# A decoder block's first stage: how the denominators of the rational softmax are inverted

## What is computed

```python
def rational_softmax(scores, eps=EPS):                     # EPS = 1e-6
    num = 0.5 * (1.0 + scores * jax.lax.rsqrt(1.0 + scores * scores))
    return num / (jnp.sum(num, axis=-1, keepdims=True) + eps)
...
scores = jnp.where(causal[None, None], NEG, scores + alibi)
probs = rational_softmax(scores, EPS)
out = jnp.einsum('bhts,bhsd->bhtd', probs, v)
out = jnp.transpose(out, (0, 2, 1, 3)).reshape(B, T, C)
return out @ w_out.T                                       # added to x
```

## Time and profile before

| | |
|---|---|
| median of three runs | 3285.65 us |
| the profiled execution | 3286.76 us |
| its span, first to last instruction | 3284.9 us |
| TensorE busy, share of the span | 3043.6 us, 93% |
| VectorE busy | 1644.6 us, 50% |
| ScalarE busy | 1347.1 us, 41% |
| GpSimd busy | 733.1 us, 22% |
| TensorE's granted clock, mean | 0.962 |

### The profile page before, as it was taken

How to read it: one execution, slowest core, us unless ns; L and a number is a source line. 1 busy time by engine, 2 the same in 40 slices (tenths; PEclk the granted TensorE clock), 3 DMA queues, 4 the chain that set the end, 5 groups by cost and what they waited for, 6 DMA issues and landing times. The chain is left out here.

```text
span 3284.9 us, 50660 instructions
## 1 busy us (share of the span) xinstructions
PE 3043.6 (93%) x19312; PEld 2491.3 (76%) x19312; DVE 1644.6 (50%) x3785; ACT 1347.1 (41%) x2298; POOL 733.1 (22%) x560
## 2 busy tenths in 40 slices
PE   6889999878999999999999959999999999999997
PEld 4667777756777777777777738888888888888886
DVE  5888888863555556555555633323233323333321
ACT  5677777764555555555555521111111111121111
POOL 0000000011112122221212124242524242424232
PEclk9889999989999999999999969999999999999999
DMA  2011111124111111111111013141414141414132
GB/s 98 23 35 46 44 37 42 45 80 132 39 38 38 44 37 51 54 37 37 38 43 37 17 48 102 52 97 52 97 52 104 51 102 52 97 52 97 52 74 36
DMA packets 93874, 189.70 MB, mean 58 GB/s; under 512 B 17568, under 2 KB 27552, under 8 KB 91712
## 3 DMA queue, kind: packets, MB, share of 16 engines
q1 hardware_dynamic: 79168, 158.68, 15.9%
q0 software_dynamic: 14592, 29.43, 5.0%
HBM read 140.25 MB, written 47.82 MB: 57 GB/s over the span
## 5 line engine op out<-in xcount | busy, mean ns | idle before, releaser
L1757 ACT ACTIVATE f_hf<-f_h 128x448 f32<-128x448 f32 x256 | 139.8, 546 | 1012.4 <-PE f_h L1784 979.7
L1728 DVE CAST f_hh<-f_hf 128x448 fp32r<-128x448 f32 x256 | 106.4, 416 | 845.3 <-ACT f_hf L1757 824.5
L1799 PE MATMUL f_y<-f_w2h,f_hh 128*128 128x512 f32 x896 | 357.4, 399 | 0.0
L1687 POOL TENSOR_TENSOR f_w1l<-f_raw,f_w1h 128x512 fp32r<-128x512 f32 x128 | 182.4, 1425 | 777.3 <-DVE f_w1h L1711 777.1
L1799 PE MATMUL f_y<-f_w2h,f_hl 128*128 128x512 f32 x896 | 354.0, 395 | 0.0
L1799 PE MATMUL f_y<-f_w2l,f_hh 128*128 128x512 f32 x896 | 352.2, 393 | 0.0
L1380 ACT ACTIVATE c_s_sb<-c_s_sb,c_nmx 112x750 f32<-112x750 f32 x256 | 236.1, 922 | 200.4 <-DVE c_nmx L1214 198.5
L1372 ACT COPY c_pT<-psum 125x672 f32<-125x672 f32 x256 | 184.8, 722 | 244.8 <-PE psum L1475 236.8
L1475 PEld LDWEIGHTS psum<-a_ident,c_s_sb 112*125 112x125 f32 x1536 | 199.2, 195 | 93.7 <-issue 88.8
L1784 PE MATMUL f_h<-f_xTh,f_w1h 128*128 128x448 f32 x1024 | 254.8, 370 | 2.9 <-DVE f_xTl L1716 1.4
L1784 PE MATMUL f_h<-f_xTl,f_w1h 128*128 128x448 f32 x1024 | 250.0, 366 | 0.0
(11 more groups left out here) (246 smaller groups left out, 5833.5 us busy)
## 6 DMA issues: line engine op xcount, KB each, us to landing
f_raw<-in_w SPq DMA_DIRECT2D x128, 512.0 KB, 4.2
h_craw<-in_ctxT SPq DMA_DIRECT2D x16, 1125.0 KB, 5.1
a_x_in<-in_x SPq DMA_DIRECT2D x9, 896.0 KB, 5.7
a_xr<-in_x SPq DMA_DIRECT2D x8, 896.0 KB, 6.0
x_dram<-a_xr SPq DMA_DIRECT2D x8, 896.0 KB, 4.8
q_dram<-a_q SPq DMA_DIRECT2D x32, 224.0 KB, 5.6
h_q<-q_dram SPq DMA_DIRECT2D x16, 448.0 KB, 5.4
c_x<-x_dram SPq DMA_DIRECT2D x16, 448.0 KB, 4.9
```

Source lines behind the costliest of these rows:

```text
L1687: pool.tensor_tensor(w1s[1][:, l % NSLOT].rearrange("p k c -> p (k c)"), raw1[:, g % 2, l % 2, :], w1s[0][:, l % NSLOT].rearrange("p k c - ...
L1728: dve.tensor_copy(hs[0][:, l % 2, c * HC:c * HC + HC], hf[:, c, :]).then_inc(h_hi, 1)
L1757: act.activation(hf[:, c, :], H[:, 0:HC], ACT.Gelu_apprx_tanh).then_inc(free, 1)
L1799: mm = pe.matmul(Y[t][:], hs[a][:, l % 2, 128 * t:128 * t + 128], w2s[b][:, l % NSLOT, :], start=j == 0 and q == 0, stop=last_of_expert(l) ...
```

## The change

ScalarE no longer approximates the reciprocal; one pass of Identity brings the denominators plus epsilon from PSUM into `rden`. VectorE takes their reciprocal with its own instruction into `dt[:, 0]` and multiplies the values by it, after a wait for the reciprocal. The output is now positive, so the residual is an addition. The semaphore `d_made` counts one per step, and `rs_made` is no longer used. `dt` keeps its size, its second half unused.

```diff
@@ output (VectorE)
             dve.wait_ge(rden_made, i * NG + n + 1)
-            dve.scalar_tensor_tensor(dt[:, 0, :], pv[:, T:2 * T], 4 * RS_EPS, rden[:], ALU.add, ALU.mult).then_inc(d_made, 1)
-            dve.tensor_tensor(dt[:, 1, :], pv[:, 0:T], rden[:], ALU.mult).then_inc(d_made, 1)
-            dve.wait_ge(d_made, i * (2 * NG) + 2 * n + 2)
-            dve.scalar_tensor_tensor(o_sb[:, n % 2, :], dt[:, 0, :], 2.0, dt[:, 1, :], ALU.subtract, ALU.mult).then_inc(o_made, 1)
+            dve.reciprocal(dt[:, 0, :], rden[:]).then_inc(d_made, 1)
+            dve.wait_ge(d_made, i * NG + n + 1)
+            dve.tensor_tensor(o_sb[:, n % 2, :], pv[:, 0:T], dt[:, 0, :], ALU.mult).then_inc(o_made, 1)
@@ residual (VectorE)
-            dve.tensor_tensor(xr[:, j, :], xr[:, j, :], gen[b][0:R, :], ALU.subtract).then_inc(gen_free[b], 1)
+            dve.tensor_tensor(xr[:, j, :], xr[:, j, :], gen[b][0:R, :], ALU.add).then_inc(gen_free[b], 1)
@@ reciprocal (ScalarE)
             act.wait_ge(pv_full, i * NG + n + 1)
-            act.activation(rden[:], pv[:, T:2 * T], ACT.Abs_reciprocal_sqrt, bias=eps[:, 2:3]).then_inc(rs_made, 1)
-            act.wait_ge(rs_made, i * NG + n + 1)
-            act.activation(rden[:], rden[:], ACT.Square).then_inc(rden_made, 1)
+            act.activation(rden[:], pv[:, T:2 * T], ACT.Identity, bias=eps[:, 2:3]).then_inc(rden_made, 1)
```

## The result

The changed kernel takes 3325.39 us (median of four runs, 3323.6 to 3326.1) against 3285.55 before (four runs): ratio 1.0122, 95% interval 1.011 to 1.0135. It is slower by 40 us; 3321 was forecast.

What follows compares the result with a forecast made beforehand. A ring of waits between ScalarE and VectorE bounds the first stage; R = 1.50 us adds 4.2 us in each of five iterations (21) and 4.5 in three (13.5), so 3286.8 + 34.5 = 3321 us, range 3296 to 3358.

Steps and rivals of the forecast that it cites:

- The ring: First stage: ScalarE and VectorE wait on each other in a loop, 9.92 us per plain step; forecast 0.81 us longer.
- The price of R: Time of VectorE's new 128x224 reciprocal in the output group: taken as 1.50 us, break-even at 0.69 us.
- the three readings of the small rows: Reciprocal's time from one- and two-element rows: 6 ns per element, 1.50 us; 10 ns, 2.39 us; fixed 5 ns extra, 0.40 us.
- step 0: First four-head group of an iteration, VectorE full with residuals of OUT2 and OUT3 beside the ring: +0.81 us.
- step 1: Second four-head group of an iteration, set by the ring with ScalarE a little late: +0.75 us.
- step 2: Third four-head group of an iteration, ScalarE 0.85 us late; longer ring 10.73 against 10.72 us now: 0.0.
- steps 3 and 4: Fourth and fifth four-head groups of an iteration, plain ring at 9.92 us: +0.81 us each.
- steps 5 and 6: Sixth and seventh four-head groups, set by TensorE at 10.42 and 10.39 us; ring becomes 10.73: +0.35 us each.
- step 7: Last four-head group of an iteration, TensorE covers about half of the longer ring: +0.35 us.
- Rival (d): TensorE's clock falls to 0.88 in mid iterations, steps 5 to 7: +2 to 3 us per iteration, 3335 us; chance 0.05.
- (a): Output group: reciprocal is an ordinary pass of 0.40 us, ring 0.29 us shorter, 3274 us; chance 0.11.
- (b): Output group: reciprocal of 0.55 to 0.9 us cancels out, ring changes under 0.2 us, 3282 to 3291 us; chance 0.06.

Runs made afterwards that it cites:

- the quarter: Changed kernel with the reciprocal of only 56 of the 224 columns, used for all four quarters; 3267.39 us, ratio 0.998 to the kernel before.
- the extra reciprocal: Changed kernel with one more 128x224 reciprocal of a constant per step on VectorE, right ahead of L486; 3339.71 us, ratio 1.0198 to the kernel before.

## Why the prediction was right

- **The ring.** It named the chain L504, L660, L641, L643, L486 to L502 and said that VectorE's idle time is in it. Shown from both sides: the 64 reciprocals cost 57 us behind L495 and 8 us ahead of L486 (ScalarE's pass taken out with them there), the longer the reciprocal the longer the plain step, and in the changed kernel a second pass on ScalarE costs nothing.
- **The price of R.** 1.50 taken, 1.546 measured; the first of the three readings of the small rows, 6 ns per element, stands against 6.25. The second (10) and the third (a fixed 5 ns) fall. That it came so close is partly luck. It halved the 12 ns by which the reciprocal of two elements (166) lies above a pass of 154. The line of the wide reciprocals has its base at 145 and gives 158 for two elements, so the base was 9 ns too high and the row 8 ns above the line, and the two errors nearly cancel. From the base of 145 the same row would have given 10.5 ns per element, near the upper end of the readings. Of the two rules of the Trainium skill, the divide with a repeat count of 8 (VectorE: DVE Perf Modes, "First, the fixed hardware budget") has the direction but not the size: an estimated 8.3 ns per element against 6.25. The other rule of the Trainium skill, the plain mode's one result per cycle (Vector Engine (DVE) Microarchitecture Reference, 5.1), doesn't hold for this instruction.
- **The sum.** Step by step, forecast against measured: step 0 +0.81, +0.87; step 1 +0.75, +0.74; step 2 0.0, +0.07; steps 3 and 4 +0.81, +0.87; steps 5 and 6 +0.35, +0.36 and +0.40; step 7 +0.35, +0.30. One iteration 4.2 against 4.48 (88.83 less 84.35). The five middle ones came to 20.4 (21 forecast); the first of them grew by 3.1 only, since one of its steps had been 11.97 us long before. So the 20.4 is near 21 because a little more per iteration met a little less in one of them.
- **What was too small**: the other three iterations, 13.5 taken. They make up the rest of the shift, 18.7 us of the 39.1 by which the last output starts later: the first iteration grew by 6.4, the second by 7.5 (with the slow step below), the last by 3.4, and the first output starts 1.4 later. The estimate of 4.5 each was no count of steps: before the change the first iteration has six of eight at 9.92 to 9.99.
- **Rival (d), the clock.** It happened, but in single steps. In step 4 of the second iteration TensorE waited 3.63 us for the output (timeline of TensorE):

```profile
202.19 0.98 PE L829 MATMUL psum<-a_ew,a_v 112*32 112x224 f32 x8 [3.63 <-DVE a_o_sb L503]
...
204.59 1.86 PE L734 MATMUL psum<-a_xTh,a_wqkvh 128*128 128x448 f32 x4
...
209.22 1.05 PE L734 MATMUL psum<-a_xTh,a_wqkvh 128*128 128x448 f32 x4
```

Four products of 448 columns took 1.86 us, four such products 4.6 us later 1.05. The windows around it:

```profile
204.00:208.00 4.00, 4.00 (x21) 3.29 (x14) 3.06 (x3) 2.75 (x3) 0.00 (x0) 0.50 0.00 0
208.00:214.00 6.00, 6.00 (x30) 5.12 (x30) 5.19 (x6) 2.28 (x5) 0.00 (x0) 0.96 0.00 0
```

The granted clock was 0.50, the level of 1.2 GHz, right behind that wait, and returned while TensorE worked on. Step 4 itself still had its 10.79 us. The price came in step 5: TensorE, now behind, worked without a pause up to 226 us, and ScalarE had to wait for its scores (timeline of ScalarE):

```profile
215.62 1.29 ACT L640 ACTIVATE a_ew<-psum 112x1344 f32<-112x1344 f32 x1 [2.38 <-PE psum L812]
```

That step was 13.27 us long, 2.5 more than its fellows. The kernel before has such a case too: in the step ahead of the one of 11.97 us (where its fellows have 10.4) four such products took 1.86 us, behind a wait of 1.88. In the mean of the middle stretch the clock stayed at 0.96, so the rival as priced, all middle iterations at 0.88, did not come.
- **Where a term failed without harm**: "ScalarE gains up to 0.39" in step 2. It is TensorE's product that holds ScalarE there, as the quarter shows. The forecast didn't lean on it (step 2 was set to the ring), but rivals (a) and (b) did.

## What to carry to other kernels

Where three engines hand one result round, ask on which side of the wait an operation stands: the same 64 reciprocals on VectorE cost 57 us behind the wait for ScalarE and 8 us ahead of it, and taking a pass from ScalarE, which waits itself, gave nothing that could be measured. Fewer passes are not less time: one reciprocal of 224 columns costs as much as four ordinary passes, so three passes were cheaper than two. And when a new instruction is only in the trace at a tiny size, tiny instructions of the same operand count give a choice of prices and no more: here they allowed 0.40 to 2.39 us, and the one taken was close partly by luck. Two runs with half and a quarter of the width gave the price.

## What the runs showed of the hardware that was not expected

- The line of the wide reciprocals (145 ns plus 6.25 per element) would give 151 and 158 ns for one and two elements; the trace has medians of 164 (from 152 to 167) and 166. Most of the small ones lie above the line, so the slope between them (2 to 3 ns) misleads.
- Reading its input from PSUM, the reciprocal takes 1558 ns, 12 more than from SBUF.
- TensorE's clock fell to half within a middle iteration too: with the extra reciprocal its mean in 240 to 690 us was 0.93 against 0.96, with two steps of 13.68 and 13.49 us among fellows of 10.8. In both TensorE had just waited 3.04 us, and the granted clock was 0.50 in 277 to 281 and in 649 to 653 us. It was 0.55 in 266 to 270 as well, behind a wait of 1.99, in a step that kept its 10.78 us.
